# Opening of a linear-attention block: first x turned by TensorE, chunk 1's norms on GpSimd, parameter rows spread by TensorE

## The reference

```
ffn(x)  = norm(norm(x)) * g + b
x1      = x  + 0.5 * ffn(x)
x2      = x1 + attention(norm(x1))      # 16 heads of 32
out     = x2 + 0.5 * ffn(x2)
attention: q, k, v = x Wq', x Wk', x Wv';  f = elu + 1
           S += f(k) v',  z += f(k);  o = f(q) S / (f(q) z + eps);  result o Wo' + bo
```

## Time and profile before

| what | us |
|---|---|
| median of 3 runs (926.61 to 927.86) | 926.72 |
| time of the profiled execution | 928.43 |
| its span | 926.7 |
| PE busy | 895.8 (97%) |
| DVE busy | 832.2 (90%) |
| ACT busy | 753.7 (81%) |
| POOL busy | 705.0 (76%) |

### The profile page before, as it was taken

One profiled execution on the slowest core, in us unless ns is written; L12 is line 12 of the kernel. 1 busy time (PEld: TensorE's weight loads), 2 busy tenths in 40 slices (PEclk: granted clock), 3 DMA queues, 4 the chain that ended last, 5 costly groups with the idle time before them and its releaser, 6 DMA issues.

```text
span 926.7 us, 29932 instructions
## 1 busy us (share of the span) xinstructions
PE 895.8 (97%) x10252; PEld 525.3 (57%) x10252; DVE 832.2 (90%) x1537; ACT 753.7 (81%) x1301; POOL 705.0 (76%) x869
## 2 busy tenths in 40 slices
PE   3999999999999999999999999999999999999995
PEld 2555555555556656555655555665555565555562
DVE  7889889899999999999999999999999999989787
ACT  5888788888888888888888888888888888888682
POOL 3268777788777789777778877778977778987672
PEclk9999999999999999999999999999999999999998
DMA  7576798766687666677767678767668776767783
GB/s 249 131 146 134 150 180 157 131 150 150 145 181 158 140 146 148 147 166 158 159 137 153 146 152 174 160 137 151 148 145 172 158 153 141 143 132 138 131 138 98
DMA packets 421564, 139.80 MB, mean 151 GB/s; under 512 B 402576, under 2 KB 402832, under 8 KB 421520
## 3 DMA queue, kind: packets, MB, share of 16 engines
q1 hardware_dynamic: 404496, 106.73, 61.2%
q10 hardware_dynamic: 17024, 32.51, 10.5%
HBM read 21.76 MB, written 16.78 MB: 42 GB/s over the span
## 4 chain that ended last, share of the span: by engine, by line
PE 87%; DMA 4%; DVE 3%; issue 3%; ACT 1%; POOL 1%; SPq 0%; DVEq 0%; ACTq 0%; POOLq 0%
PE PJ L1596 49%; PE PJ L1701 16%; PE AV L1675 8%; PE SC L1648 6%; PE AV L1687 5%; PE AV L1672 3%; DMA AT<-ATTN 2%; DMA KS<-KN 1%; DMA X<-in_L_attn_x_dram 1%; DMA shift<-in_L_ffn_ln_b_dram 1%; DVE AM L1166 1%; PE SC L1573 0%; DVE TP L1290 0%; POOL A L500 0%; POOL X1BO L433 0%
## 5 line engine op out<-in xcount | busy, mean ns | idle before, releaser
L1596 PE MATMUL PJ<-wT,XT 128*128 128x512 f16 x2304 | 526.0, 380 | 0.2
L1596 PEld LDWEIGHTS PJ<-wT,XT 128*128 128x128 f16 x2304 | 217.7, 98 | 245.1 <-issue 4.7
L500 POOL TENSOR_TENSOR A<-AM,A 128x512 f16<-128x512 f32 x252 | 288.0, 1162 | 30.4 <-ACT A L783 30.4
L1701 PE MATMUL PJ<-wT,AT 128*128 128x512 f16 x768 | 176.0, 379 | 1.2 <-DMA AT<-ATTN 1.2
L490 POOL TENSOR_SCALAR_AFFINE_SELECT AM<-AM 128x512 f32<-128x512 f32 x124 | 78.9, 636 | 114.4 <-ACT AM L770 114.4
L783 ACT ACTIVATE A<-AM 128x512 f16<-128x512 f32 x256 | 153.7, 631 | 12.0 <-POOL AM L490 9.9
L1675 PE MATMUL AV<-VN,A 128*128 128x33 f16 x3072 | 116.4, 177 | 0.0
L1701 PEld LDWEIGHTS PJ<-wT,AT 128*128 128x128 f16 x768 | 71.1, 97 | 78.8 <-DMA AT<-ATTN 2.7
L1672 PE MATMUL AV<-SS,QS 128*128 128x33 f16 x1024 | 111.7, 178 | 0.0
L1675 PEld LDWEIGHTS AV<-VN,A 128*128 128x128 f16 x3072 | 108.8, 96 | 3.7
L1166 DVE TENSOR_TENSOR AM<-SC,causal 128x512 f32<-128x512 f32 x132 | 89.8, 683 | 19.9 <-PE SC L1648 19.7
(11 more groups left out here) (113 smaller groups left out, 1520.4 us busy)
## 6 DMA issues: line engine op xcount, KB each, us to landing
out_dram<-Y ACTq DMA_DIRECT2D x31, 512.0 KB, 3.2
X<-in_L_attn_x_dram ACTq DMA_DIRECT2D x30, 512.0 KB, 3.5
X<-in_L_attn_x_dram SPq DMA_DIRECT2D x2, 512.0 KB, 7.9
A<-in_L_attn_Wk_dram SPq DMA_DIRECT2D x1, 1024.0 KB, 9.0
A<-in_L_attn_Wq_dram SPq DMA_DIRECT2D x1, 1024.0 KB, 11.2
QS<-in_L_attn_Wv_dram SPq DMA_DIRECT2D x1, 1024.0 KB, 15.5
XT<-XH SPq DMA_TRANSPOSE x64, 3.4
QS<-in_L_attn_Wo_dram SPq DMA_DIRECT2D x1, 1024.0 KB, 5.7
```

The source lines that it names most:

```text
L500: g.tensor_tensor(A[:, b, LO, hg], AM[:, k % 4], A[:, b, HI, hg], ALU.subtract).then_inc(a_lo.sem, 1)
L1596: ins = t_.matmul(PJ[b], XT[:, w, c, b * C:(b + 1) * C], wT[m_][:, m, c, :], start=(c, w, m) == todo[0], stop=(c, w, m) == todo[-1])
L1701: ins = t_.matmul(PJ[b], AT[:, b, w, c * C:(c + 1) * C], wT[3][:, m, c, :], start=(c, w, m) == todo[0], stop=(c, w, m) == todo[-1])
```

## The change

It concerns the opening alone; the loop's bodies are the same, and so is what is computed.

* Loads: SP's order becomes Wk, x tile 0, x tile 1, Wq, Wv, Wo, x of chunk 1. Gain, shift and bias come as single rows by ACT's queue, and PE spreads each over 128 partitions by a float32 matmul with a row of 0.5 (or 1.0); ACT copies them out of PSUM. DVE's two halvings go.
* Chunk 0: POOL's powers are done tile by tile; DVE normalises it instead of ACT, PE transposes it in float32 (4 transposes a tile), and ACT and DVE take the halves from the turned tile straight into XT. The DMA transposes of chunk 0 go.
* Chunk 1: POOL does x + shift, (x - mean) * rstd, times gain, their sum, the second normalisation and the low half. ACT's `front_scale` and `normalise` and DVE's `front_gain`, `front_x1` and `x_low` go for this chunk.
* W_O is turned through AV's two banks; its parts stand later in all lists. Scores of step 0 wait for 12 low parts, no longer for 16.
* `project` in the opening waits part by part for the low weights (before: for all four parts of a matrix).
* S and SS are cleared by POOL. Five transposes without use (`place_loop`) stand in PE's opening ahead of the loop.

```diff
+ def spread_row(i):   # PE
+     pe.wait_ge((gain_loaded, shift_loaded, obias_loaded)[i], 16)
+     t_.matmul(spare[i][:], (half_row, half_row, ones_row)[i][:], rows[i], start=True, stop=True).then_inc(row_spread, 1)
+ def turn_first(b):
+     pe.wait_ge(*xn_done.upto(0, b))
+     for c in range(GROUPS):
+         ins = t_.transpose(TP[b][:, c * C:(c + 1) * C], XN[:, b, c * P:(c + 1) * P], ident[:])
+     ins.then_inc(x_first_turned, 1)
+ def place_loop():
+     for _ in range(5):
+         t_.transpose(NORMS[:, 0:P], ident[:], ident[:])
  w_turn(j, c), k = 4 * j + c:
+     if 2 <= k < W_REUSE: pe.wait_ge(rows_kept, k - 1)
+     elif j == 3 and c == 1: pe.wait_ge(w_scaled, 4)
+     elif j == 3: pe.wait_ge(wT_lo, k - 1)
+ project, opening: if (w, m) == PASSES[0]: pe.wait_ge(wT_lo, W_ORDER.index(m_) * GROUPS + c + 1)
+ def keep_row(i):   # ACT
+     act.wait_ge(row_spread, i + 1)
+     a.activation((gain, shift, obias)[i][:], spare[i][:], ACT.Copy).then_inc(rows_kept, 1)
+ def normalise_first(b):   # DVE
+     v.scalar_tensor_tensor(XN[:, b], X1[:, b], stat1[:, b, 0:1], rstd1[:, b:b + 1].to_broadcast([P, E]),
+                            ALU.subtract, ALU.mult).then_inc(xn_done.sem, 1)
+ def x_shifted(b):   # POOL
+     pool.wait_ge(*x1bo_done.upto(n))
+     g.tensor_tensor(X1[:, b], X[:, 1, b], shift[:], ALU.add).then_inc(x_gained.sem, 1)
+ def x_summed(b):
+     g.tensor_scalar(X2[:, b], X[:, 1, b], stat0[:, b, 0:1], rstd0[:, b:b + 1], ALU.subtract, ALU.mult).then_inc(g0_done.sem, 1)
+     g.tensor_tensor(X2[:, b], X2[:, b], gain[:], ALU.mult).then_inc(n_gained, 1)
+     g.tensor_tensor(X1[:, b], X1[:, b], X2[:, b], ALU.add).then_inc(x1_done.sem, 1)
+ def normalise_up(b):
+     g.tensor_scalar(XN[:, b], X1[:, b], stat1[:, b, 0:1], rstd1[:, b:b + 1], ALU.subtract, ALU.mult).then_inc(xn_done.sem, 1)
+ def x_low_up(b):
+     g.tensor_tensor(XH[:, b, LO], XN[:, b], XH[:, b, HI], ALU.subtract).then_inc(x_lo.sem, 1)
```

More of the change, by code:

```diff
@@ L892, in opening @@
-                first.exp_relu_q(0)
-                first.next_x()
+                first.q_half(0)
+                w_half(2, 3)
                 first.exp_relu_q(1)
-                w_half(2, 3)
-                first.q_half(0)
-                first.normalise(0)
                 first.q_half(1)
+                first.x_half_up(0)
                 w_half(3, 0)
-                first.x_half(0)
+                second.front_scale(0)
+                second.copy_scores(0, 1)
+                first.x_half_up(1)
@@ L901, in opening @@
+                first.v_half(0)
+                second.split_a(0, 0)
+                first.v_half(1)
                 w_half(3, 1)
-                first.normalise(1)
+                second.front_scale(1)
                 w_half(3, 2)
[L904 to L911, removed]
@@ L1386, in opening @@
+                w_low(0, 0)
+                early.normalise_first(1)
+                top_norm(1)
+                w_low(0, 1)
+                scale_w(1)
+                w_low(0, 2)
+                row_sums(2)
+                early.x_low_first(0)
                 first.front_stats(0)
                 first.front_stats(1)
+                row_sums(3)
+                scale_rest(1)
+                top_norm(2)
+                w_low(0, 3)
                 first.front_mean(0)
-                row_sums(1)
@@ L1405, in opening @@
+                early.x_low_first(1)
+                second.front_stats(0)
                 w_low(1, 2)
-                top_norm(2)
-                scale_rest(1)
-                scale_w(2)
+                second.front_stats(1)
+                first.phi_k(0)
                 w_low(1, 3)
-                first.phi_k(0)
-                first.front_gain(1)
+                first.front_stats1(0)
+                first.low_k(0)
+                top_norm(3)
+                first.phi_k(1)
                 w_low(2, 0)
+                second.front_mean(0)
@@ L1446, in opening @@
                 second.mask(0, 2)
+                first.low_v(1)
+                w_low(3, 2)
+                second.front_x1(0)
+                second.mask(1, 0)
                 second.phi_k(0)
-                scale_rest(3)
+                w_low(3, 3)
                 second.front_x1(1)
+                second.phi_k(1)
                 second.front_stats1(0)
+                second.front_stats1(1)
+                second.phi_q(0)
+                second.mask(1, 2)
                 second.low_k(0)
-                second.mask(1, 0)
```

372 lines of the change are left out of this document (214 added, 158 removed).

## The result

The changed kernel takes 933.22 us (median of 4 runs, 932.71 to 935.45) beside 926.66 for the kernel before on the same chip (4 runs, 925.99 to 927.86): a ratio of 1.0074, 95% interval 1.0054 to 1.0094. It is slower by 6.6 us, where the forecast was 1.4 us faster.

The account below looks back on a forecast made before the run. PE was taken to set the loop's 27.49 us step, unchanged; only the opening moves, with step 1 starting at 56.9 instead of 58.3. So 926.72 - 1.4 = 925.3 us, range 922.5 to 927.9 (own range 924.0 to 926.7).

Parts of the forecast that it names:

- Step 1: Opening loads: Wk lands at 5.7 us instead of 11.40, x tile 0 at 6.4, tile 1 at 7.1.
- Step 2: Spread rows on PE: 0.4 to 1.7 us per float32 matmul, hidden ahead of Wk's first norm.
- Step 3: Opening up to the first projection: normalise_first 1 ends at 16.85, project_k 0 begins at 21.0, 2.1 us earlier.
- rival D: DVE and POOL exclude each other at normalise_first 1: 927.6; low_k 0 and 1 held too: 928.6 or more; chance 0.16.
- Step 4: Opening projections: project_k 0 takes 4.6 us at low clock, POOL's chunk 1 chain hidden by about 3 us, 2.4 won.
- rival C: POOL becomes the bound: at 2.36 us per tensor_scalar instead of 0.9, normalise_up 1 and ACT move 1.5 us: 926.8; chance 0.08.
- A: The forecast itself, with PE's clock still low at the start of project_k 0: 925.3 us; chance 0.42.
- B: PE's clock is up before project_k 0, which starts at 20.3 and ends at 23.6: 923.5 us; chance 0.30.
- Step 5: End of the opening: ACT waits 0.85 us for POOL at x_half_up 1; loop step 1 begins at 56.9, gain 1.4 us.
- What PE gains there, the end gains: Whatever PE gains in reaching loop step 1 (58.3 us before) reaches the kernel's end, if the other engines follow.
- Step 6: Dropped and moved work: nobody waits for chunk 0's DMA transposes, W_O through AV's banks frees scores, longer opening costs nothing.
- rival E: The loop is no longer held in instruction fetch: 16 us or more over 12 passes, 943; chance 0.04.

Follow-up runs that it names:

- e11: Changed kernel with all of chunk 1's norm arithmetic and low half back on ACT and DVE, without the edits of e1 and e5; 930.85 us, ratio 1.0061.
- e6: Changed kernel with the edits of e1, e2 and e5, and chunk 1's second norm and low half back on ACT and DVE; 926.94 us, ratio 1.0007.
- e1: Changed kernel with POOL's bias made to wait until DVE's normalise_first 1 is done; 932.28 us, ratio 1.0062.
- e2: Changed kernel with chunk 1's x1 made by ACT and DVE as before, second norm and low half still on POOL; 932.67 us, ratio 1.0078.
- e5: Changed kernel with step 0's low_k 0 moved in DVE's list from last in the opening to ahead of front_stats1 0; 932.98 us, ratio 1.0066.
- e9: Changed kernel with POOL's four tensor_scalar operations on 128 of 512 columns, and the gain multiplication reading X1; 932.28 us, ratio 1.0068.
- e10: Changed kernel with only chunk 1's second norm and low half back on ACT and DVE, x1 still on POOL; 932.28 us, ratio 1.0072.
- e12: Changed kernel with the edits of e9 and e1 together: narrow POOL operations, and POOL's bias behind normalise_first 1; 930.26 us, ratio 1.0046.
- e3: Changed kernel with the edits of e1 and e2 together; 932.21 us, ratio 1.0053.
- e7: Changed kernel with the edits of e1, e2 and e5, POOL's spread_q 0 ahead of its second norm, ACT's x_half_up 1 behind both v_half; 930.74 us, ratio 1.0037.
- e4: Changed kernel without place_loop, the five idle transposes on PE ahead of the loop; 934.05 us, ratio 1.0086.
- e8: Kernel before with one move: step 0's low_k 0 put last in DVE's opening; 927.18 us, ratio 1.0002.

## Why the prediction was wrong

**Where the loss sits.** Starts of the same work, in us:

| kernel | `project_k` 0 | q1 | load | median less before's |
|---|---|---|---|---|
| before | 23.10 | 59.34 | 163.8 | 0 |
| after | 23.99 | 62.95 | 169.5 | +6.6 |
| e11: chunk 1 off POOL | 23.79 | 61.42 | 167.7 | +5.2 |
| e6: no exclusion, `low_k` early too | 22.07 | 59.68 | 164.3 | +0.6 |

Taken back in this order, POOL's arithmetic for chunk 1 costs 1.8 us at the load, the exclusion 1.7, the late `low_k` 0 1.7, and 0.5 are left of the rest. The parts don't add up one by one. Taken out alone they gave 0.8 (e1), 0.6 (e2), 0.7 (e5), 0.3 (e9) and 0.1 (e10) at the load. Each hides another: whoever comes earlier waits for the next.

**Step 1** was late by what it had left open. W_k was there at 6.45 us, near the later of its two landing times (5.6 and 6.5), and DVE read x at 7.21, 0.8 us after the 6.4 of the sum. The whole row behind it is late by as much: e1, with no exclusion, has `project_k` 0 at 21.84 for 21.0.

**Step 2** had the price too low and the cost right. One spread row is one matmul of the program and two in the trace, 2.07 us together, above the upper bound of 1.7. The second row began at 5.19, when the shift had landed, where the forecast had it there between 2 and 4 us. It cost nothing: PE still waits 0.40 us for DVE ahead of W_k's first norm.

**Step 3, normalise_first 1 at 16.85, failed**; it ended at 19.7. This is rival D, nearly to the number: bias first, 2.35 us, an end forecast at 19.2, and `project_k` 0 at 23.3 (measured 23.99). e1 and e6 show it: with the wait the operation takes 0.75 us, and `project_k` 0 begins at 21.84 and 22.07. D's own time was 927.6, or 928.6 and more with its second part, so D alone is not the result. I gave D 0.16, because the order of the two was open to 0.1 us; the margin measured is 0.14 us (bias at 16.81, DVE at 16.95). The Trainium skill's page "SBUF — State Buffer", section "Who interferes with whom", has the rule that a DVE instruction with two SBUF inputs contends with a GpSimd instruction that reads SBUF. The traces agree where POOL's operation is a `tensor_tensor` or a copy: DVE's ends about 0.55 us after POOL's, in `normalise_first` 1 (2.76 us) as in `low_k` 0 (1.09 at 63.55). They don't agree where it is the new `tensor_scalar`. Eight times in six profiles a `low_k` began inside one, and it took 0.73 to 0.75 us, as if POOL were idle (DVE at 33.35 and POOL at 32.06, above). So D's second part, `low_k` 0 and 1 held, didn't happen in the changed kernel, and it did happen in e9, whose cheap operations moved POOL's other ones beside them.

**Step 4, the price of POOL's new operation, was mis-sized**: 2.08 us where 0.9 was taken, inside its bounds (0.64 and 2.36). The power that starts the chain also came late, at 27.2 against 24.5; 1.7 us of that is the exclusion (25.5 in e1). So x1 was complete at 36.84 (forecast 31.4), and the "hidden by about 3 us" became DVE's wait of 1.49. The choice of the nearest row was bad: a select has one input and no per-row scalars, and between ends so far apart the chain should have been worked out at the upper one for all four operations; rival C did it for one. e9 keeps this in proportion, as far as its own collisions let it.

**Step 4, the clock**: `project_k` 0 took 3.50 us, not 4.6, and 2.8 to 4.1 in the other versions of the changed kernel. That is between A and B: luck, since it varies from one execution to the next. Another change of the clock was not foreseen, and it seems to have cost the changed kernel nothing. The windows of PE (stretch, its us, busy, PEclk, DMA, GB/s) after, then of e6:
```profile
39.00:42.00 3.00, 0.65 (x3) 1.00 0.92 175
42.00:45.00 3.00, 2.50 (x7) 0.59 0.45 88
45.00:48.00 3.00, 2.24 (x16) 0.84 1.18 200
```
```profile
39.00:42.00 3.00, 1.63 (x6) 1.00 0.63 179
42.00:45.00 3.00, 2.35 (x19) 1.00 1.13 210
45.00:48.00 3.00, 3.00 (x20) 1.00 1.03 197
```
After PE's 2.47 us of waiting the granted clock falls to the lower level, and the nine matmuls at 42.67 take 3.75 us; six in e6 take 1.48, so nine would be about 2.2, 1.5 us less. The fall is in the profiles of after, e1, e5, e9, e10 and e12, and in none of e2, e3, e6, e7 and e11, where x1 is off POOL. e4 and e5 have the same lists up to here, but for the five idle transposes at 7 us that e4 lacks, and the same wait of 2.2 us, and only e5 has the fall. PE's timeline, first e4, then e5:
```profile
44.17 1.48 PE L1696 MATMUL PJ<-wT,XT 128*128 128x512 f16 x6 [0.51 <-DVE wT L1147]
...
47.77 0.61 PE L1747 MATMUL SC<-QS,KS 96*128 96x128 f16 x8 [1.68 <-DMA QS<-QN]
```
```profile
44.17 2.74 PE L1696 MATMUL PJ<-wT,XT 128*128 128x512 f16 x6 [0.47 <-DVE wT L1147]
...
47.80 0.61 PE L1747 MATMUL SC<-QS,KS 96*128 96x128 f16 x8 [0.38 <-DMA QS<-QN]
```
The fall is not certain in each execution, and its 1.3 us disappear in the wait for q's transposed tile: q1 is 63.10 without it and 63.13 with it. After's scores wait for the same tile, 0.76 us. What holds PE there is the tile, and ahead of it on POOL the second norm: e7 puts q's spread ahead of that, and the scores begin 1.0 us earlier.

**Step 5** failed by what went before. ACT's wait for POOL at `x_half_up` 1 is there, 1.06 us for 0.85. In e12, which has both assumptions, nothing waits at the scores, so there the fall of the clock can cost up to 1.3 us (six matmuls in 2.74 instead of 1.48). Without it q1 would be at 57.9 at best, 1.4 us ahead of before; that is worked out, not run. That it equals the forecast's gain is partly luck: `project_k` 0 begins 0.85 us later there than forecast, and PE waits 0.86, 1.29 and 0.49 us for DVE in `project_v` 0, where the forecast had it run through.

**"What PE gains there, the end gains"** is the sentence that failed in steps 1 to 3. I followed DVE's list to `mask(0,2)` and not to its end, so I didn't see that `low_k` 0 had moved behind two statistics, a PHI and a mask, and that SP's next transposes stand behind k's. e5, e8 and e11 against e6 show 0.9, 1.8 and 1.7 us more from q1 to the load with it, in one profile each. The forecast put nothing there.

**Step 6 and rival E.** The loop stayed held, and without the placement it is held too (e4). W_O's new banks and the other moves cost no more than the 0.5 us by which e6 is behind at the load, as far as one profile tells. e6 also shows that the gain was small to begin with: `project_k` 0 begins 1.0 us before the old one, and PE then waits 0.90, 0.50 and 0.43 us for DVE within `project_v` 0.

**The two profiles and the medians.** Spans differ by 4.3 us and medians by 6.6. From the last load to the end it is 130.7 us before and 129.3 after: the profiled execution of the kernel before had a stretch of its closing (866 to 872 us) at a granted clock of 0.72, and was 1.7 us above its median; e6's has the same stretch, and e8's, with nothing in the closing changed, has not. So I take it for chance. The profiled execution of the changed kernel was 0.5 us below its own median; with the 1.7 us that makes up the difference.

**Open.** How the cost of POOL's arithmetic splits between price and place: e2, e9 and e10 show that no single one carries it, and e7 against e6 gives the second norm 1.3 us at the load and 3.8 in the medians. Why the late `low_k` 0 costs under 1.2 us in e8's runs when its profile shows 1.8 is open too. From last load to end the profiles differ by up to 2.4 us (128.6 in e11, 131.0 in e7), and one profile a kernel can't tell how much of that is chance. No version beat the kernel before.

## What to carry to other kernels

Work taken off a full engine and given to an idle one is paid for by what stands behind it in the second engine's list: price the new operation at its upper bound over the whole chain, and look at which of DVE's operations have two SBUF inputs at that moment. Follow each in-order queue to the end of the edit; one operation moved to the end of DVE's list cost three steps about 1.7 us in the profiles, through a DMA queue. Where several small delays hide one another, undoing one shows little: take them all out, and put them back one at a time. And look in the trace at what an ablation moves: the cheap operation of e9 brought POOL's other work beside DVE's.

## What the runs showed of the hardware

- POOL's `tensor_scalar` with two per-row scalars took 2.08 us for 128x512 float32 and 0.80 for 128x128, more than a two-input operation of the same size (1.27).
- A float32 matmul that spreads one row of 512 over 128 partitions stood in the trace as two and took 2.07 us, at the start of the program.
- A DVE operation with two SBUF inputs, begun 0.14 us after POOL's `tensor_tensor` of 2.35 us, took 2.76 us in place of 0.75. Step 0's `low_k` 0 took 1.09 beside one of POOL's splits, and e12's `low_k` 1 1.53 beside a copy. Beside POOL's `tensor_scalar` of 2.08 us the same operation took 0.73 to 0.75, eight times out of eight.
- The granted clock fell to the lower level during `project_v` 0 after PE had waited (2.47 us in after, 0.86 and 1.29 in e12), in six of the seven profiles with x1 on POOL. After's came back some 3 us later. Of e4 and e5, whose lists differ up to there by five idle transposes at 7 us, it fell in e5 alone.
